# Large cross-attention: one wait for both exponents at the head of each key tile's step, and the four score products in a row

## What is computed

```python
q_big  = rope((x @ Wq.T per head) @ w_kc_q)           # 192 wide
kv_r   = rope(ctx_512)                                # 1601 keys x 64
q_r    = q_big @ W_qr ;  k_r = kv_r @ W_kr            # 64 wide per head
attn   = softmax(q_r @ k_r.T)                         # 64 queries x 1601 keys
x      = x + (((attn @ kv_r) @ w_kc_kv.T) @ Wo.T)
```

## Time and profile before

| | us |
|---|---|
| median of three runs | 3492.39 |
| the three runs | 3491.53, 3492.39, 3500.60 |
| the profiled execution | 3504.15 |
| its span, first to last instruction | 3501.60 |
| busy in the span: TensorE / VectorE / ScalarE / GpSimd | 2942.5 / 2084.2 / 1277.2 / 900.8 |
| mean granted TensorE clock | 0.932 |

### The profile page before, as it was taken

The page is one execution under the profiler, slowest core; times in us unless marked ns, Lnnn a source line. Parts: engine busy times, 40 slices in busy tenths (PEclk is TensorE's granted clock), DMA queues, the critical chain, the costliest instruction groups (busy, mean ns, idle before and its releaser), DMA issues. The chain is left out here.

```text
span 3501.6 us, 51568 instructions
## 1 busy us (share of the span) xinstructions
PE 2942.5 (84%) x17592; PEld 1773.8 (51%) x17592; DVE 2084.2 (60%) x3249; ACT 1277.2 (36%) x2482; POOL 900.8 (26%) x784
## 2 busy tenths in 40 slices
PE   6767734579988988898898889888996889999999
PEld 3544412445544544454455445444543457777776
DVE  3445567357686777677776877686775643333332
ACT  3433312123344343434334433444343333333332
POOL 0001000134354444344434544453440000000000
PEclk9888856679999999999999999999999899999999
DMA  1000030000000000000000000000003000000000
GB/s 39 0 17 0 0 117 0 22 19 10 19 9 19 9 19 9 19 9 19 9 11 17 19 9 9 19 9 19 10 0 145 0 0 0 0 0 0 0 0 25
DMA packets 15045, 57.83 MB, mean 17 GB/s; under 512 B 2512, under 2 KB 7248, under 8 KB 13584
## 3 DMA queue, kind: packets, MB, share of 16 engines
q1 hardware_dynamic: 13392, 53.57, 5.5%
q10 hardware_dynamic: 1600, 3.56, 0.3%
HBM read 55.03 MB, written 2.10 MB: 16 GB/s over the span
## 5 line engine op out<-in xcount | busy, mean ns | idle before, releaser
L917 ACT ACTIVATE cx_prob<-cx_st 128x512 f32<-128x512 f32 (+1 forms) x832 | 477.4, 596 | 742.8 <-PE cx_st L774 680.7
L645 POOL TENSOR_TENSOR cx_acc<-cx_acc,cx_prob 128x512 f32<-128x512 f32 (+1 forms) x352 | 493.8, 1403 | 751.5 <-ACT cx_prob L917 747.4
L1023 DVE TENSOR_REDUCE cx_mhalf<-cx_mx 128x1 f32<-128x804 f32 x512 | 491.2, 983 | 86.5 <-PE cx_mx L747 83.7
L785 PE MATMUL cx_av<-cx_prob,cx_kv 128*64 128x512 f32 (+1 forms) x1664 | 462.2, 635 | 0.0
L773 PE MATMUL cx_st<-cx_q,cx_k 128*128 128x512 f32 (+1 forms) x832 | 372.5, 448 | 84.5 <-ACT cx_prob L917 60.5
L1506 PE MATMUL moe_gu<-moe_wgu,moe_xnT 128*128 128x352 f32 x1280 | 399.0, 463 | 0.0
L1044 DVE TENSOR_TENSOR cx_acc<-cx_acc,cx_prob 128x512 f32<-128x512 f32 (+1 forms) x352 | 371.3, 1055 | 21.7 <-ACT cx_prob L917 19.9
L747 PE MATMUL cx_mx<-cx_k,cx_q 128*128 128x402 f32 x1024 | 309.3, 388 | 53.2 <-DVE cx_mhalf L1023 47.3
L1641 DVE SCALAR_TENSOR_TENSOR moe_hid<-moe_silu,moe_coef,moe_gu 128x176 f32<-128x176 f32 x320 | 127.1, 397 | 351.6 <-ACT moe_silu L1569 349.4
L774 PE MATMUL cx_st<-cx_q,cx_k 128*128 128x512 f32 (+1 forms) x832 | 332.8, 400 | 0.0
L747 PEld LDWEIGHTS cx_mx<-cx_k,cx_q 128*128 128x128 f32 x1024 | 173.4, 195 | 264.0 <-DVE cx_mhalf L1023 216.8
(11 more groups left out here) (214 smaller groups left out, 3945.0 us busy)
## 6 DMA issues: line engine op xcount, KB each, us to landing
cx_ctx<-in_cx_ctxT SPq DMA_DIRECT2D x32, 402.0 KB, 4.3
cx_ctxr<-in_cx_ctxrT SPq DMA_DIRECT2D x32, 402.0 KB, 5.5
moe_wgu<-in_moe_wgu SPq DMA_DIRECT2D x5, 1408.0 KB, 15.3
moe_wd<-in_moe_wd SPq DMA_DIRECT2D x4, 896.0 KB, 25.0
x_all<-in_x SPq DMA_DIRECT2D x1, 2048.0 KB, 5.3
cx_wq<-in_cx_wq SPq DMA_DIRECT2D x1, 2048.0 KB, 12.0
cx_woT<-in_cx_woT SPq DMA_DIRECT2D x1, 2048.0 KB, 29.5
out_x<-x_all SPq DMA_DIRECT2D x1, 2048.0 KB, 7.5
```

The costliest lines, as they stand in the source:

```text
L645: pool.tensor_tensor(acc[0][rows, :], sofar, prob[slot(kt)][rows, 0, :], ALU.add)\
L785: last = pe.matmul(av[DCX * p:DCX * p + DCX, :], kv[e][0:nk(kt), kt, :], prob[slot(kt)][0:nk(kt), p, :], start=(kt == 0), stop=(kt == NKT ...
L917: act.activation(prob[slot(kt)][rows, p, :], st[p][rows, :], ACT.Exp).then_inc(s_exp, 1)
L1023: dve.tensor_reduce(mhalf[:, i // 2, i % 2:i % 2 + 1], mx[i % 2][:, :, 0:KQ], AX.XY, ALU.max)\
```

## The change

The wait for exponents moves to the head of the step and asks for both halves of tile kt; the two score products S0 and S1 follow it directly; V has no wait on exponents of its own, except in the very last step of the last batch, where no scores stand ahead of it. Everything else keeps its place, so the order becomes S0 S1 X0 X1 V X2.

```diff
-            def scores(n, e, kt, p):
+            def scores(n, e, kt):
                 keys = slice(kt * P, kt * P + nk(kt))
-                g = 2 * kt + p
-                if not (is_first(n) and g < 2):
+                if not (is_first(n) and kt == 0):
 
-                    pe.wait_ge(s_exp, n * 2 * NKT + g - 1)
-                if g == 0:
+                    pe.wait_ge(s_exp, n * 2 * NKT + 2 * kt)
+                if kt == 0:
 
                     pe.wait_ge(s_rowk, 2 * n + 2)
-                pe.matmul(st[p][0:nk(kt), :], k1[e][:, keys], q1[e][:, p, :, :], start=True, stop=False)
-                pe.matmul(st[p][0:nk(kt), :], k2[e][:, keys], q2[e][:, p, :, :], start=False, stop=True)\
-                    .then_inc(s_st, 1)
-
-            def values(n, e, kt):
-                pe.wait_ge(s_exp, n * 2 * NKT + 2 * kt + 2)
+                for p in range(2):
+                    pe.matmul(st[p][0:nk(kt), :], k1[e][:, keys], q1[e][:, p, :, :], start=True, stop=False)
+                    pe.matmul(st[p][0:nk(kt), :], k2[e][:, keys], q2[e][:, p, :, :], start=False, stop=True)\
+                        .then_inc(s_st, 1)
+
+            def values(n, e, kt, waited):
+                if not waited:
+                    pe.wait_ge(s_exp, n * 2 * NKT + 2 * kt + 2)
...
                     for third in range(3):
                         if third == 2:
-                            values(n, e, kt)
-                        elif kt + 1 < NKT:
-                            scores(n, e, kt + 1, third)
-                        elif next:
-                            scores(n + 1, 1 - e, 0, third)
+
+                            values(n, e, kt, kt + 1 < NKT or next)
+                        elif third == 0 and kt + 1 < NKT:
+                            scores(n, e, kt + 1)
+                        elif third == 0 and next:
+                            scores(n + 1, 1 - e, 0)
```

More of the change, by code:

```diff
@@ L817, in before @@
                 max_rows(0, 1)
-                scores(0, 0, 0, 0)
-                scores(0, 0, 0, 1)
+                scores(0, 0, 0)
             def batch(n, t, e, more, next):
```

## The result

The changed kernel takes 3517.64 us, the median of six runs (3509.76 to 3523.95), against 3496.57 us for six runs of the kernel before on the same chip. The ratio is 1.0057, with a 95% interval of 1.0036 to 1.0078: slower by 0.57%, some 20 us. The forecast was 3496.5 us and the range ended at 3513; the measured time lies outside it.

What follows compares the result with a forecast made beforehand. TensorE, nearly always working in the attention, was taken as the bound, with few waits to win or lose. 15 odd batches at 0.26 us, taken as 4 us, on the median 3492.39 gave 3496.5 us; range 3484 to 3513.

Steps and rivals of the forecast that it cites:

- V's wait: Attention, 416 V: removing the satisfied wait taken at 0; a rival put 0.08 us each, 33 us gained, chance 0.05.
- the +0.48: Even batch, step 1: S0 goes 0.48 us later, waiting for half 1; the delay is hidden before L802.
- the later additions of steps 5 to 9: Even batch: X0 pieces 0.48 us later, but VectorE's addition still ends after GpSimd's; taken as 0.
- the queries: Odd batch, steps 0 to 4: 0.28 us gained in step 0, 0.16 in step 4; step 5's copies start 0.44 sooner.
- I take half, 0.26: Odd batch: of the 0.52 us shift a pair, half is given back by the clock; ends 0 and 0.83.
- the path shift at 0.52: Odd batch, step 5: first piece 0.52 us later, at 1687.34 against 1686.82, and this arrives at L760.
- upper end: Odd batch, step 5: GpSimd's addition goes first at the shared ports, VectorE's ends later, +0.83 us a pair.
- TensorE's clock as a buffer: Odd batch, S0 of step 5 to L760: a 1.2 GHz stretch costs 0.97 us; part of 0.52 can be given back.
- rival 1: Even batch, step 1: wait of 2.24 us brings a second slow stretch, 9 to 15 us on top, about 3508; chance 0.25.
- the path's upper end (3505): Whole kernel: 15 odd batches at 0.83 us each on 3492.4 us give 3505.
- Rival 2: Even batch: the 0.32 us cover fails and VectorE's chain takes the 0.48, 7 us lost, 3504; chance 0.06.
- Rival 4: Odd batch: the slow stretch disappears while the 0.52 shift stays whole, -7 us, 3485.5; chance 0.07.

Runs made afterwards that it cites:

- experiment 4: Kernel before, with V's wait on exponents left out wherever a score product stands ahead of it in the same step: 3488.40 us, ratio 0.9984.
- experiments 5 and 6: Kernel before with unread matmuls in its long waits; 5: S0 waits for half 1 everywhere, 1.0002; 6: order S0 S1 X0 X1 V X2, old waits, 1.0002.
- experiment 10: Kernel before with S1 directly behind S0 in the odd batch's steps 0 to 4 only, no unread matmuls: 3498.02 us, ratio 0.9983.
- experiment 3: Kernel before, with S0 of the even batch's step 1 waiting for half 1 instead of half 0: 3513.31 us, ratio 1.0037.
- experiment 1: Kernel before, with unread matmuls ahead of TensorE's long waits in the attention: 3479.12 us, ratio 0.9934.
- experiment 2: Changed kernel with unread matmuls (7, 8 and 4) in its longer waits; against the kernel before: 3501.99 us, ratio 1.0007.
- experiment 8: Changed kernel with unread matmuls in its long waits and GpSimd's four odd-batch rotations moved to steps 3 and 4: 3504.88 us, ratio 1.0011 to the kernel before.

## Why the prediction was wrong

**The mechanism of the path was right in the main.** The waits came out as forecast, 2.23 us at the even S0 (2.24 forecast) and 2.46 at the odd one (2.5):

```profile
970.68 0.51 PE L773 MATMUL cx_st<-cx_q,cx_k 128*128 128x512 f32 x1 [2.46 <-ACT cx_prob L918]
...
971.72 0.90 PE L747 MATMUL cx_mx<-cx_k,cx_q 128*128 128x402 f32 x4
972.29 1.90 DVE L1024 TENSOR_REDUCE cx_mhalf<-cx_mx 128x1 f32<-128x804 f32 x2 [1.89 <-PE cx_mx L747]
...
973.54 1.27 POOL L645 TENSOR_TENSOR cx_acc<-cx_acc,cx_prob 128x512 f32<-128x512 f32 x1
...
974.11 1.25 DVE L1045 TENSOR_TENSOR cx_acc<-cx_acc,cx_prob 128x512 f32<-128x512 f32 x1
...
981.75 0.99 DVE L1024 TENSOR_REDUCE cx_mhalf<-cx_mx 128x1 f32<-128x804 f32 x1 [1.11 <-PE cx_mx L747]
```

The first piece stands 1.04 us behind S0 (1.05 forecast). V's wait cost nothing (experiment 4). In the even batch the +0.48 vanished before L803, and the later additions of steps 5 to 9 cost nothing (24.18 against 24.19). In the odd batch the queries gained 0.54 (0.44 forecast) and the gate took 0.48 of it.

**The first failing step is "I take half, 0.26".** The sum put the path shift at 0.52 a pair, which supposes that VectorE's addition keeps its turn ahead of GpSimd's, took half of that off for the clock, and kept 0.83, with the turn lost, as an upper end. The trace above shows the turn lost, just as the upper end had it: GpSimd at 973.54, VectorE 0.57 us later with 1.25 us instead of 0.94, against 1091.19, 1091.76 and 1093.01 in the forecast, and in the order that the earlier trace rows had the other way round. The Trainium skill, SBUF — State Buffer, section "SBUF: two separate sides", had said that whichever starts first keeps the ports for its instruction; the trace agrees, at the odd batch's first pieces as in experiments 5 and 6. Nothing in that arithmetic was undecided, and it should have been the value and not the bound. The path shift was 0.66 to 0.71, less than 0.83 because the queries gained 0.54 instead of 0.44 and the first reduction came 0.42 us later behind S0 and not 0.48. Over 15 pairs this is 10 us where I took 3.9: 3.9 of the difference is the halving, the other 2 the lost turn.

The delay reached L760 by another way than the forecast's, which let it pass through VectorE alone. VectorE won the 0.31 back at its next addition (0.85 us against 1.16). But TensorE's pieces had by then waited for the late reductions: S0 of step 7 comes 9.47 us behind that of step 5, against 8.74 before, and VectorE waits 1.11 us for a piece (last row above) where it had waited 0.34. From there to L760 the delay stays at 0.7.

**The second is "TensorE's clock as a buffer".** I had seen that the pairs of before are even although one stretch falls in each, and concluded that the stretch would give back half of a shift. It gave back nothing: with the longer waits came more and dearer stretches, 0.68 us a pair on top in the thirteen pairs. A buffer it was only for a gain: in experiment 10 the stretches took the whole 0.54 us by which the path had become shorter. The loss is rival 1, in a wider form. It said that the even S0's wait of 2.24 us might be followed by a stretch, at 0.59 to 0.97 us each; the trace shows such a stretch at 0.97 us (1128.75), in six of thirteen pairs, and experiment 3 shows that this wait alone is enough to make the kernel slower. What rival 1 didn't have is that stretches then also come behind L760 in nine pairs of thirteen instead of two, though its wait had not changed, at 1.5 us each; these nine are 14 of the 24 us that all stretches cost in thirteen pairs.

**The third is the composition.** I held the path's upper end (3505) and rival 1 (3505 to 3511) to be alternatives, with rival 1 on top of the middle of the sum. They have different causes and came together: in the traces the attention grew by 10 us of path and 6 of clock. The range reached to 3513 because nothing in it added the two. The rest of the miss is no mechanism. The forecast stood on 3492.39, the median of three runs, and six runs gave 3496.57; with that base its range would have ended at 3517.2, and 3517.64 lies hardly beyond it. And 3496.6 + 16 = 3513 is 5 us under the measured median, which the interval of the ratio (13 to 27 us) allows.

Rival 2 (cover in the even batch) did not come at full clock, though one sign of it did: behind a stretch at the even S0, S0 to L803 takes 14.65 us against 13.68, the whole 0.97. The cover of 0.32 us that the earlier trace rows showed was not enough for that, though in experiment 3 three such stretches cost nothing. Rival 4 was the opposite of what the clock did.

**What stays open.** Why a stretch follows L760 in one pair and not in the next was not settled; the waits have equal lengths to 0.02 us in both, and experiments 3 and 10 moved the stretches without changing L760's wait. Nor was it tried whether fewer unread matmuls would do. The step from experiment 1 to 2 in the medians is 23 us. In their profiled executions the attention differs by 15.8: 0.71 x 15 = 11 of path and three stretches of 1.6 us in experiment 2. The other 7 are open; I don't know what the other runs of experiment 2 looked like inside.

## What to carry to other kernels

A wait that the previous wait on the same engine already covers cost nothing that could be measured (experiment 4); what such a change really does is move the others, and these are to be costed. Where two engines share ports, work out from the rows who starts first after the change, and take the answer as the value of the sum (here it was a lead of 0.57 us, forecast and measured; in experiments 5 and 6 a lead of 0.10 to 0.14 was enough). A wait on TensorE has two prices, its length and the slow clock behind it; add the second to a path shift instead of letting it absorb a loss (here it absorbed only a gain), and where waits of about 2 us can't be avoided, matmuls that nobody reads may pay for themselves (0.66% here), as may work of the partner engine moved to steps in which it is idle.

## What the hardware showed unexpectedly

- A 3.4 us stretch at 1.2 GHz cost from nothing to 1.7 us by its place: nothing behind the even S0 in three pairs of experiment 3, 0.53 behind the odd S0 after the change, 0.95 there before it, 1.55 behind L760, 1.7 behind L802 in experiment 8. That the second is cheap because TensorE soon waits for VectorE anyway was not tried.
- A wait lengthened by 0.48 us, off the path to within 0.04 us a pair, raised the slow time from 64 to 118 us in the traces.
- With a lead of 0.10 us for GpSimd, VectorE's addition took 1.7 us; with a lead of 0.35 to 0.4 for VectorE it took 0.94 to 0.97. Two edits that each cost VectorE the lead cost 1.26 to 1.28 us a pair, alone or together.
- Three kernels, the kernel before from its third pair on, experiment 4 and experiment 10, average 119.47 us a pair, though the path of the last is 0.55 us shorter at full clock. Why they meet there was not tried.
